# Token stage of a cross-attention kernel: weight splitting taken off GpSimd, context pieces and evictions reordered

## What is computed

```python
x = x + _L0_xattn_ref(_layernorm(x), ctx_2048, ...)
# inside it
q  = _ln(fp8_linear(ln_out, wq));  k = _ln(fp8_linear(ln_out, wk));  v = fp8_linear(ln_out, wv)
qx = _ln(fp8_linear(ln_out, wqx))
kvx = einsum('bsi,oi->bso', cond, w_kv_x)        # cond: 8 x 1601 x 512, the context
kx, vx = split(kvx);  kx = _ln(kx)
cat = concat(_gqa(q, k, v), _gqa(qx, kx, vx))    # softmax attention, 8 groups of 128 columns
return einsum('bsi,oi->bso', quantised(cat), wproj) * scales
```

## Time and profile before

| | |
|---|---|
| median of 3 runs | 1951.18 us (1949.89 to 1954.2) |
| the profiled execution's own time | 1956.55 us |
| its span | 1955.2 us |
| busy | PE 97%, PEld 82%, DVE 57%, ACT 49%, POOL 32% |
| token stage, first item's matmul to last | 18.2 to 136.4 us |
| one step of the group loop | about 24.6 us |

### The profile page before, as it was taken

One profiled execution on the slowest core, in us unless ns is written; L12 is line 12 of the kernel. 1 busy time (PEld: TensorE's weight loads), 2 busy tenths in 40 slices (PEclk: granted clock), 3 DMA queues, 4 the chain that ended last, 5 costly groups with the idle time before them and its releaser, 6 DMA issues.

```text
span 1955.2 us, 30912 instructions
## 1 busy us (share of the span) xinstructions
PE 1887.6 (97%) x10129; PEld 1602.5 (82%) x10129; DVE 1115.2 (57%) x2969; ACT 954.9 (49%) x1956; POOL 631.4 (32%) x742
## 2 busy tenths in 40 slices
PE   7899999999999999999999999999999999999879
PEld 5777888888888888888888888888888888875357
DVE  7764565645564556456655665566556655546853
ACT  6653454545554555445544554455445544435611
POOL 4235543322232223233333333343333333201010
PEclk9999999999999999999999999999999999999979
DMA  7674354534453454435453544354435433465020
GB/s 277 225 250 133 113 153 130 164 113 144 149 170 113 127 166 152 132 90 180 123 156 115 173 125 150 112 175 148 141 113 179 153 113 102 153 239 178 3 86 22
DMA packets 220209, 280.68 MB, mean 144 GB/s; under 512 B 60874, under 2 KB 123595, under 8 KB 220051
## 3 DMA queue, kind: packets, MB, share of 16 engines
q1 hardware_dynamic: 209410, 277.73, 45.0%
q10 hardware_dynamic: 8592, 0.54, 0.3%
q0 software_dynamic: 2048, 0.43, 0.1%
HBM read 238.85 MB, written 39.22 MB: 142 GB/s over the span
## 4 chain that ended last, share of the span: by engine, by line
PE 72%; POOL 5%; issue 5%; DVE 4%; DMA 3%; ACT 3%; SPq 1%; ACTq 0%; POOLq 0%; DVEq 0%
PE u_ps L615 8%; PE u_ps L616 8%; PE kx_ps L511 8%; PE u_ps L617 8%; PE kx_ps L509 8%; PE kx_ps L513 8%; PE t_ps L600 4%; PE sc_ps L586 2%; PE ssq_ps L528 2%; PE sc_ps L587 2%; PE sc_ps L588 2%; PE t_ps L641 2%; DMA stage<-in_ctx_n 1%; PE t_ps L624 1%; DMA scratch_wv_s<-wv_lo 1%
## 5 line engine op out<-in xcount | busy, mean ns | idle before, releaser
L509 PE MATMUL kx_ps<-ctxT_hi,wk_hi 128*128 128x400 f32 (+1 forms) x1024 | 363.7, 355 | 5.8 <-DVE ctxT_lo L290 5.8
L511 PE MATMUL kx_ps<-ctxT_lo,wk_hi 128*128 128x400 f32 (+1 forms) x1024 | 355.1, 347 | 0.0
L513 PE MATMUL kx_ps<-ctxT_hi,wk_lo 128*128 128x400 f32 (+1 forms) x1024 | 353.7, 345 | 0.0
L615 PE MATMUL u_ps<-ctxN_hi,pt_hi 128*128 128x512 f32 (+1 forms) x832 | 342.5, 412 | 2.7 <-DVE pt_lo L839 2.7
L616 PE MATMUL u_ps<-ctxN_lo,pt_hi 128*128 128x512 f32 (+1 forms) x832 | 330.6, 397 | 0.0
L617 PE MATMUL u_ps<-ctxN_hi,pt_lo 128*128 128x512 f32 (+1 forms) x832 | 329.1, 396 | 0.0
L839 DVE TENSOR_TENSOR pt_lo<-t_ps,pt_hi 128x512 fp32r<-128x512 f32 (+1 forms) x256 | 144.7, 586 | 252.6 <-ACT pt_hi L1089 252.6
L1058 ACT ACTIVATE kx_hi<-kx_ps 128x400 fp32r<-128x400 f32 (+1 forms) x256 | 129.0, 504 | 305.0 <-PE kx_ps L513 303.4
L1089 ACT ACTIVATE pt_hi<-t_ps 128x512 fp32r<-128x512 f32 (+1 forms) x256 | 125.8, 522 | 264.4 <-PE t_ps L600 264.4
L766 DVE TENSOR_TENSOR kx_lo<-kx_ps,kx_hi 128x400 fp32r<-128x400 f32 (+1 forms) x256 | 146.7, 573 | 174.9 <-ACT sq L1060 174.3
L821 DVE CUSTOM_DVE_ANT_0 prob<-sc_ps,rstd_bc 128x400 f32<-128x400 f32 (+2 forms) x256 | 136.5, 571 | 140.2 <-PE sc_ps L588 140.2
(11 more groups left out here) (282 smaller groups left out, 3497.8 us busy)
## 6 DMA issues: line engine op xcount, KB each, us to landing
rstd_bc<-scratch_rstd SPq DMA_DIRECT2D x64, 804.0 KB, 6.0
stage<-in_ctx_t SPq DMA_DIRECT2D x96, 267.0 KB, 4.5
stage<-in_ctx_n SPq DMA_DIRECT2D x96, 256.0 KB, 6.2
wk_hi<-scratch_wk_s SPq DMA_DIRECT2D x56, 256.0 KB, 3.0
wk_lo<-scratch_wk_s SPq DMA_DIRECT2D x56, 256.0 KB, 3.4
wv_hi<-scratch_wv_s SPq DMA_DIRECT2D x56, 256.0 KB, 4.7
wv_lo<-scratch_wv_s SPq DMA_DIRECT2D x56, 256.0 KB, 5.6
scratch_own_rows<-out_sb SPq DMA_DIRECT2D x32, 256.0 KB, 2.7
```

What stands on the lines that cost most here:

```text
L509: PE.matmul(kx_ps[:, j % 2, 0:w], wk_hi[:, g % 2, i, :], ctxT_hi[:, i, c0:c0 + w], start=(i == 0), stop=False)
L511: PE.matmul(kx_ps[:, j % 2, 0:w], wk_hi[:, g % 2, i, :], ctxT_lo[:, i, c0:c0 + w], start=False, stop=False)
L513: mm = PE.matmul(kx_ps[:, j % 2, 0:w], wk_lo[:, g % 2, i, :], ctxT_hi[:, i, c0:c0 + w], start=False, stop=(i == C - 1))
L615: PE.matmul(u_ps[:], pt_hi[0:w, t % 2, cols], ctxN_hi[0:w, y, :], start=(y == 0), stop=False)
```

## The change

1. In the token stage POOL does no weight work. Chunk 3 of `w_hi` goes to ACT; ACT now makes chunks 0 and 1 in item t=0 and chunks 2 and 3 in item t=1, in both behind the eviction of a key chunk. The first three `wk` splits go to DVE (`less_wk`, `low_wk`) and ACT (`high_wk`, four activations of 128 columns).
2. Pieces 10 and 11 are split in item 11 on both engines.
3. DVE's `keys_low` comes ahead of `weights_low` within an item.
4. In step n=-1 pieces 22 to 24 are all split behind the last key chunk, and SP issues the loads of 23 and 24 ahead of `load_rstd`.
5. Some sums, loads and stores of `wk` move to later items; POOL's waits in `split_wk` are written for the new counts; `query_stats` gets a wait on DVE's own earlier work.

```diff
+    def less_wk(self, n):
+        V = self.core.DVE
+        V.wait_ge(self.wk_summed, n + 1)
+        V.tensor_scalar(self.wk_less[:], self.wk_mean[:], -1.0 / P, None, ALU.mult).then_inc(self.wk_neg, 1)
+
+    def high_wk(self, n):
+        A, hi = self.core.ACT, self.wk_hi[:, n % 2, :, :]
+        A.wait_ge(self.wk_neg, n + 1)
+        after(A, self.kx_done, 4 * (n - 1))
+        after(A, self.wk_kept[n % 2], 32 * (n // 2))
+        for c in range(self.C):
+            ins = A.activation(hi[:, c, :], self.wk_raw[:, c, :], ACTF.Identity, bias=self.wk_less[:, c:c + 1])
+        ins.then_inc(self.wk_high, 1)
+
+    def low_wk(self, n):
+        V, hi, lo = self.core.DVE, self.wk_hi[:, n % 2, :, :], self.wk_lo[:, n % 2, :, :]
+        V.wait_ge(self.wk_high, n + 1)
+        for c in range(self.C):
+            ins = V.scalar_tensor_tensor(lo[:, c, :], self.wk_raw[:, c, :], self.wk_less[:, c:c + 1], hi[:, c, :].bitcast(F32),
+                                         ALU.add, ALU.subtract)
+        ins.then_inc(self.wk_split, 1)
...
-                whose, at, left = 0, {3: 2, 5: 2, 6: 2, 7: 1}, range(PIECES - 7, PIECES)
+                whose, at, left = 0, {3: 2, 5: 2, 7: 3}, range(PIECES - 7, PIECES)
...
-        first_high = {0: range(0, 5), 6: range(5, 7), 7: range(7, 8), 9: range(8, 10), 12: range(10, 12)}
+        first_high = {0: range(0, 5), 6: range(5, 7), 7: range(7, 8), 9: range(8, 10), 11: range(10, 12)}
         first_low = {2: range(0, 1), 3: range(1, 3), 6: range(3, 5), 7: range(5, 7), 8: range(7, 8), 10: range(8, 10),
-                     14: range(10, 12)}
+                     11: range(10, 12)}
...
                 V.wait_ge(q_in[m % 2], 32 * (m // 2 + 1))
+                after(V, q_mvd, m)
...
             for i in range(ITEMS):
                 n, t = divmod(i, 4)
+                if i - 1 in first_keys:
+                    keys_low(*first_keys[i - 1])
                 if n + 1 < NB:
                     after(V, product_done, 4 * n)
                     for c in ((0,), (1, 2, 3), (), ())[t]:
                         weights_low(n + 1, c)
-                if i - 1 in first_keys:
-                    keys_low(*first_keys[i - 1])
...
-                if i in (1, 8, 20):
-                    x.mean_wk((1, 8, 20).index(i))
+                if i in (1, 13, 22):
+                    x.mean_wk((1, 13, 22).index(i))
+                    x.less_wk((1, 13, 22).index(i))
+                if i in (4, 16, 25):
+                    x.low_wk((4, 16, 25).index(i))
...
             scale_tokens(0, 0)
+            weights_high(0, 3)
             feat.scalar(2, lnT, feat_ps, "ln_w", "ln_b")
...
-                if n + 1 < NB and t == 0:
-                    for c in range(3):
-                        weights_high(n + 1, c)
                 if i == 20:
                     squares_out(0)
                 if i - 1 in first_keys:
...
                     keys_high(*first_keys[i - 1])
+                if n + 1 < NB and t < 2:
+                    for c in range(2 * t, 2 * t + 2):
+                        weights_high(n + 1, c)
                 for k in first_high.get(i, ()):
                     x.high(0, k)
+                if i in (2, 14, 23):
+                    x.high_wk((2, 14, 23).index(i))
...
-            G.wait_ge(scales_set, 5)
-            weights_high(0)
             for i in range(ITEMS):
-                n, t = divmod(i, 4)
-                if n + 1 < NB and t == 1:
-                    weights_high(n + 1)
-                if i in (1, 9, 21):
-                    x.split_wk((1, 9, 21).index(i))
...
-                if i == 14:
+                if i == 18:
                     x.load_wk(2)
                     x.keep_wk(1)
...
                 refill(0, 1)
+                if n == -1:
+                    refill(3, 4)
                 if n + 2 < N:
                     load_rstd(n + 2)
                 if n >= 0 and not odd and u + 1 < N // 2:
                     load_own(u + 1)
-                refill(3, 4)
+                if n >= 0:
+                    refill(3, 4)
```

More of the change, by code:

```diff
@@ L307, in split_wk @@
         G.wait_ge(self.wk_summed, n + 1)
-        after(G, self.wk_centred, n)
+        G.wait_ge(self.wk_split, n)
         G.tensor_scalar(self.wk_less[:], self.wk_mean[:], -1.0 / P, None, ALU.mult).then_inc(self.wk_neg, 1)
@@ L312, in split_wk @@
                         ALU.add).then_inc(self.wk_centred, 1)
-        G.wait_ge(self.wk_centred, n + 1)
+        G.wait_ge(self.wk_centred, n - 2)
         after(G, self.kx_done, 4 * (n - 1))
@@ L417, in attend @@
         x_in, scales_set, w_in = [sem(f"x_in{t}") for t in range(4)], sem("scales_set"), [sem("w_in0"), sem("w_in1")]
-        hi_act, hi_pool, lo_done = sem("w_hi_act"), sem("w_hi_pool"), sem("w_lo_done")
+        hi_act, lo_done = sem("w_hi_act"), sem("w_lo_done")
         product_done, out_act, out_dve = sem("product_done"), sem("out_act"), sem("out_dve")
@@ L770, in weights_low @@
                 sc = blocks[n][1]
-                if c < 3:
-                    V.wait_ge(hi_act, 3 * n + c + 1)
-                else:
-                    V.wait_ge(hi_pool, n + 1)
+                V.wait_ge(hi_act, 4 * n + c + 1)
                 V.scalar_tensor_tensor(w_lo[n % 2][:, c, :], w_raw[:, n % 2, c, :], w_sc[:, 4 * sc + c:4 * sc + c + 1],
@@ L1234, in gpsimd @@
         def gpsimd():
-            def weights_high(n):
-                sc = blocks[n][1]
-                G.wait_ge(w_in[n % 2], 16 * (n // 2 + 1))
-                after(G, product_done, 4 * (n - 1))
-                if n == 1:
-                    G.wait_ge(feat.turned, 4)
-                G.tensor_scalar(w_hi[n % 2][:, 3, :], w_raw[:, n % 2, 3, :], w_sc[:, 4 * sc + 3:4 * sc + 4], None,
-                                ALU.mult).then_inc(hi_pool, 1)
             def split_wv(n):
```

## The result

The changed kernel takes 1946.19 us (median of 7 runs, 1944.06 to 1948.47), the kernel before 1951.73 in the same comparison (7 runs, 1949.68 to 1955.53). The ratio is 0.9963, with the interval 0.9954 to 0.9972: 7.2 us faster (5.5 to 9.0), where 6.95 was forecast. 1944.2 was predicted in the range 1939.5 to 1949.0. The profiled execution of the changed kernel took 1948.47 us with a span of 1947.1, 8.1 us less than the span before.

The account below looks back on a forecast made before the run. PE, busy 97% of the span, was taken as the bound. Item 16 −4.1, key_squares +0.5, B +0.4, clock +2.5 and D −6.25 gave −6.95 us, taken from the median 1951.18: 1944.2 us, range 1939.5 to 1949.0.

Parts of the forecast that it names:

- D: Step 0, PE's wait at key_squares(2) on ACT's squares: earlier loads remove 3.7 us idle plus 2.55 slow clock, −6.25 us.
- rival 1: Token stage: DVE catches up and the clock stays up, −9.5 to −11.2 us, 1940.0 to 1941.7; chance 0.25.
- rival 2: Transfers late: all 2.8 us reach ACT, item 12 waits about 1.5; −5.3 to −2.5 us in all; chance 0.20.
- Item 16: Token stage: with pieces 10 and 11 earlier, item 16 starts at 60.5 instead of 64.56, set by DVE's chain; −4.1 us.
- POOL's work goes, so I give DVE its undisturbed durations: about 3 us: DVE's chain before item 16: without POOL's weight splitting beside it, its instructions lose their surplus, about 3 us.
- The clock: Before item 16: 3.3 us of remaining PE idle time brings a spell of lower clock, +2.5 us (0 to 3.3).
- B: PE's 0.9 us wait at the start of block 8: the third low_wk on DVE lengthens it by about 0.4 us.
- key_squares(0): Waits about 0.5 us because ACT is late with keys_high(0, 3) in item 18, behind high_wk(1).
- The late piece 5: Its load, behind item 2's store on SP, is issued later and delays ACT by 0.7 us (0 to 2.8).
- rival 3: Step 0: the earlier loads don't remove the wait, only the token part's −0.7 us remains, 1950.5; chance 0.08.
- The short activations: Four 128-column wk instructions take about 1.2 us for high_wk on ACT, 1.1 for low_wk; the first is hidden.
- Rival 4: Slower: ACT's late high parts delay each of 11 block starts, 1.1 us each, +12 us, 1956; chance 0.05.

Follow-up runs that it names:

- e2: Changed kernel with part 4, the earlier transfers of pieces 22 to 24, undone; 0.9988 of the kernel before, 2.3 us faster.
- e3: Kernel before with only pieces 10 and 11 split in item 11 on both engines; 0.9979 of the kernel before, 4.1 us faster.
- e1: Kernel before with part 4 alone (pieces 22 to 24, loads 23 and 24 ahead of load_rstd); 0.9981, 3.7 us faster.
- e8: Kernel before with parts 2 and 4, the edits of e1 and e3, together; 0.9962 of the kernel before, 7.4 us faster.
- e7: Changed kernel with pieces 10 and 11 put back in items 12 (ACT) and 14 (DVE); 0.9969 of the kernel before, 6.1 us faster.
- e11: Token moves of e10 made on the kernel of e8, where GpSimd keeps its weight work; 0.9958 of the kernel before, median 1944.96 us.
- e4: Kernel before with parts 2, 3 and 4, GpSimd keeping its weight work; 0.9964 of the kernel before, median 1946.8 us.
- e10: Changed kernel with key tokens scaled in item 5, rounded in 7 and 10, last query tokens' second half one item later; 0.9937, median 1941.8 us.
- e6: Changed kernel with DVE's keys_low put back behind weights_low; 0.9958 of the kernel before.
- e5: Changed kernel with key tokens scaled in item 5 and rounded in items 7 and 12; 0.9945 of the kernel before, 10.7 us faster.

## Why the prediction was right, and where it was not

The forecast held by its time: −7.2 us in the runs (5.5 to 9.0), −6.95 predicted. By its steps it held less well, and two of its errors cancel: D was counted too high and the token stage too low. (Its bounds are rounded outwards: its own sums give 1940.0 for rival 1 and 1948.7 for rival 2.)

**D, −6.25: right in its way, right in that profile, too large as a price.** The loads are issued ahead of the scale's load (143.53 against 148.34 in the changed kernel), ACT and DVE no longer stand, values(0, 0) ends and key_squares(2) starts right behind it, and the stretch is 6.35 us shorter. POOL's slack at keys(3, 0) was put at 0.9 us; its split ends at 162.65 and PE comes at 163.72, 1.07. What failed is the step "D costs 3.7 + 2.55", which sized D in an execution 5.4 us slower than the median and then took it from the median. The wait hangs on a round trip: sums of squares out and back, POOL's power, the scale out and back, and the same code gave 3.70, 1.95 and 2.34 us of wait in the kernel before, e2 and e3, with and without a spell behind it: 6.35, 3.6 and 2.4 us in all. In the profile of the kernel before two of the trip's parts were long:

```profile
142.32 0.27 POOL L1286 TENSOR_SCALAR var_col<-ssq_col 128x13 f32<-128x13 f32 x1 [2.03 <-DMA ssq_col<-ssq_sb]
142.67 3.00 POOL L1289 TENSOR_TENSOR rstd_col<-var_col,minus_half 128x13 f32<-128x13 f32 x1
```

In e1 the same two are 1.07 and 2.46; in e2 and e3 the first is 1.24 and 0.93, the second 2.46. What D costs in most executions the profiles can't say: those of e2 and e3 are faster than their medians, by 2.5 and 2.8 us, as that of the kernel before is slower. The timed runs have the step three times: 3.7 us (e1, 1.8 to 5.5), 3.3 (from e3 to e8) and 4.9 (from e2 to the change). The first leaves 6.25 out; the other two cross comparisons and are as uncertain as their size.

**Item 16, −4.1: −3.5, or −3.85 from item 8.** The place, the cause and the length of the chain were right (15.4 us predicted, 60.95 − 45.39 = 15.6 found), and the pieces are the cause (e7, e3). The wait there came out at 2.44 and not 3.3, because item 16 came 0.55 us later than forecast (61.05) and PE was through with keys(0, 2) 1.4 us later (58.61 in place of 57.2). Of the 1.4, 0.34 were lost by item 8, to the late rise of the clock and not to the change; 0.2 up to item 12; and 0.56 at item 15 on DVE's output, which I had not counted. The step "POOL's work goes, so I give DVE its undisturbed durations: about 3 us" is right on the durations and wrong as a reason for gain: the same edit that removed 2.6 us of disturbance put the wait of 2.76 us on ACT into the chain, and e3, with neither, is as fast. Both were in the prediction, the late start at 45.1 and the 3 us saved, but it never set one against the other.
The Trainium skill, "SBUF — State Buffer", section "Who interferes with whom", has a DVE instruction with two SBUF inputs and a GpSimd instruction that reads SBUF contend. The runs agree in kind: in e11 three low parts take 3.21 us with GpSimd at work and 2.07 a block later, from 56.62, when GpSimd is idle. Whether the relief pays depends on DVE's queue: nothing that can be told (the change against e8), 0.8 us in the profiles (against e4), 4.1 timed (e10 against e11, parts 3 and 5 included).

**The clock, +2.5: +1.4, and by chance.** A spell did follow item 16, one of 3.4 us and not of 6.8. Compared with the stretch from item 16 to item 32 in e2, which had no spell (42.55 against 43.98), it cost 1.4 us. The bound of 0 was as near: e2 has the same code up to there, waits 2.06 us at item 16 and has no spell. Rival 1's clock was one execution away.

**B, +0.4, and key_squares(0), +0.5: both 0.** Block 8 waits 0.88 us as before. low_wk took 1.13 us, as estimated, but it stands where DVE before waited 1.47 us for ACT's squares, and the low part of block 7 behind it still waits 0.84 for its high part (1.38 before). key_squares(0) starts after about 0.1 us.

**The late piece 5, +0.7 (0 to 2.8): 1.0 in this profile, which other executions don't bear out.** Its load is issued at 32.60 in place of 28.36, 3.0 us later counted from the first item, and ACT has it at 38.80, 1.0 later: 6.2 us from issue to use, where it was 8.2. Two thirds of the delay were made up. But e2, e6 and e7 issue it 12.2 to 12.7 us behind the first item (10.2 in the profile before), and ACT has it at 17.2 to 17.7, sooner than the 18.35 of the profile before. So the term is about nothing, and its agreement luck. Rival 2 is out: item 12 lost 0.2 us and not 1.5. So is rival 3, since the loads did go ahead.

**The short activations: right.**

```profile
30.45 1.28 ACT L315 ACTIVATE wk_hi<-wk_raw,wk_less 128x128 fp32r<-128x128 f32 x4 [1.19 <-DVE wk_less L307]
31.63 0.58 ACT L1198 ACTIVATE out_sb<-t_ps 128x512 f32<-128x512 f32 x1
```

Four take 1.28 us, 0.30 each from start to start (1.2 estimated), and the output behind them starts at 31.63; no item waits for its bank. The estimate from the Trainium skill, "ScalarE: Activation LUTs", section "What ACT_TABLE_LOAD costs", was 0.29 each. Rival 4 is out: of the eleven block starts only those of blocks 3 (0.2 us), 4 and 8 come late, and the last did so before.

The sum, then. The forecast had −6.25 for D and −0.7 for the token stage. The runs have 3.3 to 4.9 us for D, and the two profiles −2.15 for the token stage (−3.85 to item 16, +1.7 behind it). Together that is −5.45 to −7.05, against 5.5 to 9.0 timed. So part of the agreement is luck: D was 1.4 to 3.0 us too large, the token stage 1.4 too small. The two parts timed alone give −3.7 (e1) and −2.3 (e2), together −6.0, and the pieces alone −4.1 (e3), with e1's −7.8. Nothing need be missing, but the intervals would hide 1 to 2 us.

The 1.1 us behind the third part of values are within what executions differ by there. That stretch takes 1786.9 (e4) to 1791.7 us (e11) over the twelve profiles, and those two kernels have the same code there. One place is between 1679 and 1692 us, where PE waits 1.7 us for ACT in every profile: ten of the twelve have a spell there, e1 and e4 none. The changed kernel and e4, with the clock third from the right:

```profile
1675.00:1695.00 20.00, 17.31 (x79) 13.99 (x77) 10.94 (x34) 9.46 (x18) 10.74 (x12) 0.83 0.51 167
1675.00:1695.00 20.00, 16.60 (x85) 13.29 (x84) 10.66 (x32) 9.35 (x18) 10.61 (x11) 1.00 0.42 135
```

In the same way e7's 6.1 us are no riddle. Its interval, 3.9 to 8.2, holds what D alone is worth, and its profile, with gap A of full size, is its slowest run, at a granted clock of 0.984 where its other six have 0.985 to 0.989. How large gap A is in those six is open.

## What to carry to other kernels

Take the interference of two engines and the waits of the slower one together: time that an engine stops losing is worth something only if it doesn't stand at another's result next, so ask in the same breath what it will wait for once it is faster. Where a gap hangs on a round trip through memory, look at it in more than one execution before pricing it; here the same code gave 6.35, 3.6 and 2.4 us. And price a removed gap by what is late next: here three edits in a row (e3, e5, e10) each uncovered one such thing, and only the last had next to nothing left (0.65 us at item 13). Last, compare two kernels by a stretch that starts at an event near the change, and check that the clock was the same up to it.

## What the runs showed of the hardware that was not expected

- Idle time of about 2 us may or may not bring the lower clock. Of nine stretches of 1.95 to 2.51 us in which PE was idle, in the token stage and step 0, six were followed by a spell at 1.2 GHz and three were not, at almost the same length: 2.42 us at item 16 of e8 was, 2.42 at the same item of e4 was not. After 1.50 us (e5) and 0.9 there was none; after 3.70 us and more (the kernel before, e1, e7) there always was one. But the length of one wait does not settle it: the 1.7 us between 1679 and 1692 us, with shorter waits around it, came with a spell in ten profiles of twelve. Spells were 3.4 or 6.8 us long in the first 170 us; one of 3.4 cost 1.4 us at item 16. Here are e4's stages, to be held against those of the changed kernel above (PE stood until 61.89):

```profile
60.00:64.00 4.00, 2.11 (x9) 1.79 (x10) 4.00 (x7) 2.68 (x5) 0.00 (x0) 1.00 0.34 104
64.00:68.00 4.00, 4.00 (x21) 3.68 (x21) 3.93 (x7) 1.20 (x2) 0.00 (x0) 1.00 1.02 322
```

- Beside GpSimd a DVE instruction is slowed, differently by form: L206 goes from 1.22 to 1.59 us, three low parts from 2.07 to 3.21 or 3.61, the clamp from 0.42 to 1.52. GpSimd pays too. Its steps in e3, where DVE was at work beside them, and in e4, where DVE waited for ACT until 44.70:

```profile
42.79 1.40 POOL L311 TENSOR_TENSOR wk_raw<-wk_raw,wk_less 128x512 f32<-128x512 f32 x1
44.27 1.81 POOL L316 TENSOR_SCALAR wk_hi<-wk_raw 128x512 fp32r<-128x512 f32 x1
```

```profile
42.49 1.04 POOL L311 TENSOR_TENSOR wk_raw<-wk_raw,wk_less 128x512 f32<-128x512 f32 x1
43.62 1.49 POOL L316 TENSOR_SCALAR wk_hi<-wk_raw 128x512 fp32r<-128x512 f32 x1
```

- Executions of the same code differ in three places that can be named. The first load of the tokens, for which DVE waits, lands at different times: PE's first wait is 8.2 to 10.4 us over the twelve profiles, and everything behind it moves by as much. The clock rises 3.5 to 6.1 us behind the first item, and item 8 moves by 1.3 us with it. And the stretch from the third part of values in step 0 to the end varies by 4.8 us; the two extremes, e4 and e11, have 34 and 51 us at the lower clock in it.
